# All input projections of the later batches in the first sixteen steps of a Mamba recurrence

## The reference

```python
zxbcdt = x @ in_proj_w.T            # 512 -> 2688 = z 1024, x 256, B 256, C 1024, dt 128
dt = softplus(dt_in @ dt_proj_w.T + dt_proj_b)
dA = exp(dt[..., None] * A)         # 1024 channels x 16 states
def step(h, inp):                   # over 512 tokens
    h = dA_i * h + dBx_i            # dBx = dt * x * B
    y = einsum('bgn,bgcn->bgc', C_i, h)
y = (ys + D_skip * x_full) * silu(z)
return y @ out_proj_w.T
```

## Time and profile before

| | us |
|---|---|
| median of 3 runs (lowest, highest) | 2873.14 (2871.67, 2876.65) |
| the profiled execution | 2876.27 |
| its span in the trace | 2874.5 |
| busy PE / DVE / ACT / POOL | 2651.7 / 2129.6 / 1152.1 / 1255.9 |
| recurrence, first to last scan's end | 78.05 to 1062 |

### The profile page before, as it was taken

One profiled execution on the slowest core, in us unless ns is written; L12 is line 12 of the kernel. 1 busy time (PEld: TensorE's weight loads), 2 busy tenths in 40 slices (PEclk: granted clock), 3 DMA queues, 4 the chain that ended last, 5 costly groups with the idle time before them and its releaser, 6 DMA issues.

```text
span 2874.5 us, 32445 instructions
## 1 busy us (share of the span) xinstructions
PE 2651.7 (92%) x11096; PEld 1880.8 (65%) x11096; DVE 2129.6 (74%) x2731; ACT 1152.1 (40%) x1690; POOL 1255.9 (44%) x836
## 2 busy tenths in 40 slices
PE   7888888888899878999999999999989999999999
PEld 3443444444344326788887777887877788888887
DVE  4999999999999985543366677777767865555563
ACT  4555555555555534432244443443333322222221
POOL 2789888888889871110010023222212522222220
PEclk8998998989889769999999999999999999999999
DMA  6654654554465436221111112112111111111111
GB/s 230 209 157 121 188 157 121 157 166 129 132 183 154 133 99 231 81 76 49 52 66 59 45 37 67 44 45 67 44 37 45 44 49 48 51 45 52 50 47 66
DMA packets 152310, 275.35 MB, mean 96 GB/s; under 512 B 27345, under 2 KB 27857, under 8 KB 151633
## 3 DMA queue, kind: packets, MB, share of 16 engines
q1 hardware_dynamic: 152144, 273.27, 31.5%
HBM read 178.01 MB, written 61.34 MB: 83 GB/s over the span
## 4 chain that ended last, share of the span: by engine, by line
PE 71%; DVE 11%; ACT 9%; issue 5%; POOL 2%; DMA 1%; SPq 1%; DVEq 0%; POOLq 0%; ACTq 0%
PE ps L1733 19%; PE ps L1734 18%; PE ps L1735 18%; PE ps L1772 8%; DVE state L1358 6%; ACT ps L847 5%; PE ps L1784 4%; POOL read L1172 1%; DMA uraw<-y_d 1%; PE ps L1924 1%; PE ps L1868 1%; PE ps L1898 1%; DVE drive L1349 1%; DVE act_o L1677 0%; POOL xhr L1217 0%
## 5 line engine op out<-in xcount | busy, mean ns | idle before, releaser
L1172 POOL TENSOR_TENSOR read<-state,c_t 128x512 f32<-128x512 f32 x512 | 664.0, 1308 | 138.2 <-DVE state L1358 118.5
L1358 DVE TENSOR_TENSOR_SCAN state<-ps,drive 128x512 f32<-128x512 f32 x512 | 622.3, 1216 | 14.3 <-ACT ps L847 12.8
L1733 PE MATMUL ps<-xh,ghi 128*128 128x512 f32 x1536 | 609.1, 397 | 5.7 <-issue 5.7
L1231 POOL TENSOR_TENSOR wdeq<-packed,scales 128x1024 f32<-128x1024 f16 x96 | 260.2, 2711 | 798.3 <-DVE packed L1510 798.3
L1735 PE MATMUL ps<-xh,glo 128*128 128x512 f32 x1536 | 599.3, 390 | 0.0
L1734 PE MATMUL ps<-xl,ghi 128*128 128x512 f32 x1536 | 599.2, 390 | 0.0
L847 ACT ACTIVATE ps<-ps,a_exp 128x512 f32<-128x512 f32 x512 | 338.9, 662 | 473.8 <-PE ps L1772 472.5
L1772 PE MATMUL ps<-dpack,sel 128*128 128x512 f32 x512 | 260.9, 510 | 114.2 <-DVE state L1358 112.1
L1677 DVE TENSOR_TENSOR act_o<-act_o,ps 128x512 f32<-128x512 f32 x192 | 131.7, 686 | 313.4 <-PE ps L1735 298.5
L1349 DVE TENSOR_TENSOR drive<-ps,b_t 128x512 f32<-128x512 f32 x512 | 344.1, 672 | 12.7 <-PE ps L1772 11.9
L1099 ACT ACTIVATE ahi<-act_o 128x512 fp32r<-128x512 f32 x192 | 121.4, 632 | 562.6 <-DVE act_o L1677 562.6
(11 more groups left out here) (204 smaller groups left out, 3775.3 us busy)
## 6 DMA issues: line engine op xcount, KB each, us to landing
whi<-w_d SPq DMA_DIRECT2D x63, 256.0 KB, 4.1
wlo<-w_d SPq DMA_DIRECT2D x63, 256.0 KB, 4.6
dpack<-dh SPq DMA_DIRECT2D x64, 128.0 KB, 3.8
dpack<-dl SPq DMA_DIRECT2D x64, 128.0 KB, 3.6
b_d<-ev SPq DMA_DIRECT2D x32, 256.0 KB
x_d<-ev SPq DMA_DIRECT2D x32, 256.0 KB, 2.6
vpack<-vh SPq DMA_DIRECT2D x64, 128.0 KB, 3.5
vpack<-vl SPq DMA_DIRECT2D x64, 128.0 KB, 2.8
```

What stands on the lines that cost most here:

```text
L1172: pool.tensor_tensor(read[:, n % RRING, :], state[:, n % SRING, :], c_t[:, g % 2, :], ALU.mult).then_inc(read_ready, 1)
L1231: pool.tensor_tensor(wdeq[:, :].rearrange("p (h n) -> p h n", h=2), codes, scale, ALU.mult).then_inc(deq, 1)
L1358: dve.tensor_tensor_scan(state[:, n % SRING, :], ps[:, n % 2, :], drive[:, n % DRING, :], 0.0, ALU.mult, ALU.add)\
L1733: pe.matmul(out_, w_h, x_h, start=(start and k == 0), stop=False)
```

## The change

`step_jobs` now gives each of the steps 0 to 15 five jobs, counted through all batches: step g has jobs 6 + 5g to 10 + 5g, step 15 the last three. Job i of a step is done in a slot of three states, 3i to 3i+2, with one, one and two feature blocks (`slot_of`); only state 15 has none. `take` comes in the state after the slot, `w_high` in its second and `w_low` in its third. In SP's order the five weight loads and spills (`weights`, `keep`) are put between the step's other loads. x is scaled and split for batches 1 to 3 in steps 1, 5, 9 and 2, 6, 10. Tile 0 of batches 1 to 3 goes the way of the others, through `ev` to DRAM (`dt_d`); SP loads it back into `dt_in` (`load_dt_in`), and ACT and DVE split it in steps 6, 14 and 22 (`take_dt`, `dt_split`). `sp_rest` takes the room of `sp_abs`, and `soft_abs` waits for `sp_sum_ready` in turn.

```diff
@@ -40,6 +40,9 @@
...
 STEPS = B * CT
+LEAD_JOBS, STEP_JOBS = 6, 5
+DT_STEP = tuple(CT * b - 2 for b in range(B))
+SCALE_STEP, SPLIT_STEP = (None, 1, 5, 9), (None, 2, 6, 10)
 IN_TILES = 21
@@ -108,10 +111,11 @@
...
     sp_abs = place("sp_abs", [P, S], F32, after())
+    sp_rest = place("sp_rest", [P, S], F32, offset_of["end"] - 4 * S)
     sp_pos = place("sp_pos", [P, S], F32, after())
...
     sp_log = place("sp_log", [P, S], F32, after())
-    sp_rest = place("sp_rest", [P, S], F32, after())
+    dt_in = place("dt_in", [P, S], F32, after())
     dt_t = place("dt_t", [P, S], F32, after())
@@ -202,6 +206,7 @@
...
     b_d = nc.dram_tensor("b_d", [CT, P, T], F32, kind="Internal").ap()
+    dt_d = nc.dram_tensor("dt_d", [P, T], F32, kind="Internal").ap()
     y_d = nc.dram_tensor("y_d", [CT, P, T], F32, kind="Internal").ap()
@@ -219,7 +224,8 @@
...
         consts_ready = sem("consts_ready")
-        x_loaded = [sem(f"x_loaded{b}") for b in range(B)]
+        x_loaded = [None] + [sem(f"x_loaded{b}") for b in range(1, B)]
+        dt_in_loaded = sem("dt_in_loaded")
@@ -355,19 +361,19 @@
...
-            nb, k = divmod(g + 2, CT)
-            return nb, k, nb < B and k < IN_TILES // 3
-        def spills(tile):
-            return 0 if tile == 0 else 4 if tile in (X0, B0, X1, B1) else 1
+            first = LEAD_JOBS + STEP_JOBS * g
+            return first, max(0, min(STEP_JOBS, IN_TILES * B - first))
+        def slot_of(c):
+            return divmod(c, 3) if c < 3 * STEP_JOBS else (STEP_JOBS, 0)
+        def spills(job):
+            return 0 if job == 0 else 4 if job % IN_TILES in (X0, B0, X1, B1) else 1
...
-            return 16 * sum(spills(j % IN_TILES) for j in range(job % 3, job + 1, 3))
-        def taken_count(job):
-            return job - job // IN_TILES
+            return 16 * sum(spills(j) for j in range(job % 3, job + 1, 3))
@@ -485,15 +491,17 @@
...
                 nb, tile = divmod(job, IN_TILES)
-                if tile == 0:
+                if job == 0:
                     return
-                sp.wait_ge(job_taken, taken_count(job))
+                sp.wait_ge(job_taken, job)
                 if tile in (X0, X1):
...
                     dsts = [b_copies[at:at + 8, rep, :, cols(nb)] for rep in range(4)]
+                elif tile == 0:
+                    dsts = [dt_d[:, cols(nb)]]
                 elif tile >= Z0:
@@ -525,13 +533,20 @@
...
-                sp.wait_ge(job_taken, taken_count(X0))
+                sp.wait_ge(job_taken, X0)
                 for e_ in range(4):
...
                 sp.dma_start(res_d[:, :, cols(b)], hat(b)).then_inc(res_stored, 16)
+            def load_dt_in(nb):
+                job = IN_TILES * nb
+                sp.wait_ge(spilled[job % 3], spill_count(job))
+                if nb >= 2:
+                    sp.wait_ge(dtlo_ready, nb)
+                sp.dma_start(dt_in[:, :], dt_d[:, cols(nb)]).then_inc(dt_in_loaded, 16)
@@ -616,8 +631,17 @@
...
             for g in range(STEPS):
-                nb, k, jobs = step_jobs(g)
-                first = IN_TILES * nb + 3 * k
+                first, jobs = step_jobs(g)
+                more = g + 1 < STEPS
+                def weights(i):
+                    if i < jobs:
+                        weights_after(first + i)
+                def keep(i):
+                    if i < jobs:
+                        spill(first + i)
                 if g == STEPS - 3:
@@ -626,27 +650,30 @@
...
                     store_hat(g // 2)
-                if 0 <= g + 1 < STEPS:
+                if g + 1 in DT_STEP[1:]:
+                    load_dt_in(DT_STEP.index(g + 1))
+                if more:
                     load_b(g + 1)
-                if jobs:
-                    weights_after(first)
-                    spill(first)
-                if 0 <= g + 1 < STEPS:
+                weights(0)
+                keep(0)
+                if more:
                     load_c(g + 1)
+                weights(1)
                 if g >= 1:
                     store_y(g - 1)
-                if jobs:
-                    weights_after(first + 1)
-                if 0 <= g + 1 < STEPS:
+                keep(1)
+                weights(2)
+                if more:
                     load_pack_dt(g + 1)
+                keep(2)
+                if more:
                     load_pack_v(g + 1)
-                if jobs:
-                    spill(first + 1)
+                weights(3)
+                keep(3)
                 if g + 2 < STEPS:
                     load_x(g + 2)
-                if jobs:
-                    weights_after(first + 2)
-                    spill(first + 2)
+                weights(4)
+                keep(4)
             store_y(STEPS - 1)
@@ -786,9 +813,7 @@
...
                 bank = ps[:, 5 + job % 2, :]
-                if tile == 0:
-                    if nb:
-                        act.wait_ge(dtp_ready, CT * nb)
+                if job == 0:
                     act.activation(dthi[:, :], bank, ACT.Copy).then_inc(dthi_ready, 1)
@@ -797,10 +822,16 @@
...
+            def take_dt(nb):
+                act.wait_ge(dt_in_loaded, 16 * nb)
+                act.wait_ge(dtp_ready, CT * nb)
+                act.activation(dthi[:, :], dt_in[:, :], ACT.Copy).then_inc(dthi_ready, 1)
             def soft_abs(q):
...
                     act.wait_ge(sp_exp_ready, q)
+                    act.wait_ge(sp_sum_ready, q)
                 act.activation(sp_abs[:, :], ps[:, 7, :], ACT.Abs, bias=dt_bias[:, q % CT:q % CT + 1])\
@@ -901,25 +932,27 @@
...
             for g in range(STEPS):
-                nb, k, jobs = step_jobs(g)
-                first = IN_TILES * nb + 3 * k
+                first, jobs = step_jobs(g)
                 for c in range(NST):
+                    i, part = slot_of(c)
                     decay(g, c)
                     for b in (1, 2, 3):
-                        if g == CT * b - 5 and c % 4 == 1:
+                        if g == SPLIT_STEP[b] and c % 4 == 1:
                             split_hi(b, c // 4)
+                        if g == DT_STEP[b] and c == 2:
+                            take_dt(b)
                     if g == STEPS - 3 and c >= 8 and c % 2 == 1:
                         out_weights_high((c - 8) // 2)
-                    if jobs and c % 4 == 2 and c < 12 and first + c // 4 + 2 < IN_TILES:
-                        w_high(first + c // 4 + 2)
-                    if jobs and c % 4 == 2 and c > 4:
-                        take(first + c // 4 - 1)
+                    if part == 0 and 1 <= i <= jobs:
+                        take(first + i - 1)
+                    if part == 1 and i < jobs and first + i + 2 < IN_TILES:
+                        w_high(first + i + 2)
                     if 0 <= g + 1 < STEPS:
...
                             v_high(g + 1)
-                    if nb < B:
+                    if g + 2 < STEPS:
                         if c == 12:
@@ -1327,7 +1360,7 @@
...
                 dve.wait_ge(dthi_ready, nb + 1)
-                dve.tensor_tensor(dtlo[:, :], ps[:, 5 + (IN_TILES * nb) % 2, :],
+                dve.tensor_tensor(dtlo[:, :], dt_in[:, :] if nb else ps[:, 5, :],
                                   dthi[:, :].bitcast(F32), ALU.subtract).then_inc(dtlo_ready, 1)
@@ -1409,26 +1442,26 @@
...
             for g in range(STEPS):
-                nb, k, jobs = step_jobs(g)
-                first = IN_TILES * nb + 3 * k
+                first, jobs = step_jobs(g)
                 for c in range(NST):
+                    i, part = slot_of(c)
                     if c + 1 < NST:
...
                     for b in (1, 2, 3):
-                        if g == CT * b - 6 and c % 4 == 1:
+                        if g == SCALE_STEP[b] and c % 4 == 1:
                             scale_x(b, c // 4)
-                        if g == CT * b - 5 and c % 4 == 2:
+                        if g == SPLIT_STEP[b] and c % 4 == 2:
                             split_lo(b, c // 4)
+                        if g == DT_STEP[b] and c == 5:
+                            dt_split(b)
                     if g >= 1 and c == 6:
                         skip_y(g - 1)
-                    if jobs and c % 4 == 3 and c < 12 and first + c // 4 + 2 < IN_TILES:
-                        w_low(first + c // 4 + 2)
-                    if nb and jobs and k == 0 and c == 6:
-                        dt_split(nb)
-                    if nb < B and c == 15:
+                    if part == 2 and i < jobs and first + i + 2 < IN_TILES:
+                        w_low(first + i + 2)
+                    if g + 2 < STEPS and c == 15:
                         soft_rest(g + 2)
@@ -1746,10 +1779,10 @@
...
                     if job >= 2:
-                        if (job - 2) % IN_TILES == 0:
-                            pe.wait_ge(dtlo_ready, nb + 1)
+                        if job == 2:
+                            pe.wait_ge(dtlo_ready, 1)
                         else:
```

(13 more changed lines are left out.)

## The result

| | kernel before | changed kernel |
|---|---|---|
| median (lowest to highest), 6 runs each | 2873.05 (2870.55 to 2876.65) | 2882.44 (2880.1 to 2888.81) |
| ratio, 95% interval | 1 | 1.0034 (1.0022 to 1.0046) |
| profiled execution, its span | 2876.27, 2874.5 | 2881.29, 2879.5 |
| DVE busy | 2129.6 | 2135.2 |
| recurrence: DVE waits | 27.2 | 25.9 |

The change costs 9.4 us, 0.3%. The two profiled executions are 5.0 us apart; from the first scan to the end of the last one the recurrence takes 4.2 us more (988.3 against 984.1).

A forecast was written before the change was run, and what follows sets the result against it. It took DVE to bound the recurrence, PE rearrangement being worth at most some 33 us. First stretch -0.6 (14.4 lost against 15) and second stretch +1 gave about 0, so 2873 us; range 2859 to 2888.

The forecast's parts named there:

- the bursts: Steps 3, 4, 7 and 8: four-fold X or B spills ahead of deadlines lose 8 us, between 2 and 18.
- the DVE work "kept" at nothing: Batches 1 to 3: scaling and splitting x keep their DVE cost and only change steps; nothing charged.
- the light steps: Steps 16 to 29, without projections: lose 16 us against 15 before, so +1 us, between -5 and +6.
- the step's floor of 28.68 us: One recurrence step on DVE: 14 states at 1.714 us, plus 2.37 (skip row) and 2.31 (softplus row).
- PE keeps up at five jobs, the clock holds: Steps 0 to 15: PE needs 27.1 us a step at full clock; a regular step stalls 0.14 us.
- Rival D: Clock falls in state 15 all the same, so the next step's start stalls; slower, 2882 us, chance 0.08.
- v's load in regular steps: Load of v for the next step, its deadline 1.4 us earlier: 0.2 us x 12 steps = 2.4 us lost.
- edits taken at nothing: Small changes charged no time, among them the dt tile's trip through DRAM, moved x work, new waits and sp_rest.
- two deadlines: DMAs queued behind SP: the load of v for the next step, and the weights of the step's fifth tile.
- second slow gather: Light steps: half have a second, making 1.5 us a step instead of 0.74; 1.15 taken.
- the 15 regained: Steps 0 to 15: PE's gain from removing stalls, 12.4 us idle and some 2.5 hidden.
- light steps at full clock: Rival E: spreads alone keep PE's clock up in steps without projections; faster, about 2857 us, chance 0.02.

The follow-up runs named there:

- e3: Changed kernel plus three matmuls without use in every state that has no projection in steps 15 to 31; 2872.07 us.
- e4: Kernel before, with its own schedule, plus three matmuls without use in every state that has no projection; 2844.98 us.
- e7: Changed kernel with four jobs a step instead of five, so steps 0 to 19 have projections in states 0 to 11; 2888.51 us.
- e1: Changed kernel with x and B tiles of batches 1 to 3 stored once, not four times, leaving part of the output wrong; 2867.76 us.
- e6: Changed kernel with x's scaling and splitting moved to late states and the split of dt to state 13 of the step before; 2879.79 us.
- e5: Kernel before with three useless matmuls in every state without a projection, and x's scaling and splitting moved to late states; 2842.39 us.

## Why the prediction was wrong

It gave 2873, no change, 42%; slower by over 0.2% had 28%. The time lies in its range, but it is slower. Two terms of the sum failed on the slow side: the bursts, put at 8 us, cost 17.5, and the DVE work "kept" at nothing took 5.1 more. A third, the light steps, failed on the other side and hid 7 us of that. By its own steps:

- **What bounds the recurrence, and the step's floor of 28.68 us: right.** Undisturbed steps of e3 and e4 take 28.65 to 28.66.
- **PE keeps up at five jobs, the clock holds: right.** Predicted 0.14 us of stall in a regular step; steps 11 and 12 take 28.77 and 28.83. Rival D (the clock falls in state 15) is out, and that its 2882 is the measured time is chance. In e7 four states without a projection are enough to bring the stall back in twelve of twenty steps; nothing between one and four was run.
- **v's load in regular steps, 2.4 us: too high.** It cost nothing there.
- **The bursts, 8 us within 2 to 18: the mechanism right, the size wrong.** They cost 17.5, at the far end. Steps 3 and 4 cost 9.5, not 6: issues behind the stores took longer too (1.2 and 2.1 us for 0.6). Steps 7 and 8 were to lose 2 at v's load and lost almost nothing there (0.2). But steps 8, 9 and 13 lost 8.0 at a deadline that the prediction didn't list: the weights for tiles 1 and 2 of the next step, behind the four-fold spills of jobs 3 and 4 (tiles are counted from 0 within a step). In step 13 the load of `dt_in`, one of the edits taken at nothing, stands in front as well. How much of the 2.9 us is its own no run separates; e1 leaves it in and has no wait there. The prediction named two deadlines of five; every load of the step stands behind some spill. e1 shows that the waits come from the four-fold stores: without them they are gone.
- **"Scaling and splitting keep their DVE cost": wrong.** DVE's busy time grew by 5.1 us, against nothing in the sum. The page's busy shares of DVE and GpSimd were both read, but not what they do to each other. The term was there to be read: scaling took 852 to 1095 ns in the kernel before, and takes 724 in e6's late states, where GpSimd is idle. That these 5.1 us count in full in the time is not shown: e6, which took part of them away, was faster by less than the intervals can tell.
- **Light steps, +1 us: wrong in sign.** They were put at 1.15 us a step, half of them with a second slow gather, and cost some 0.6: in five of fourteen only hidden tenths of a microsecond, in the other nine one stall after state 4, never one after state 12. The stretch lost some 9 us where it had lost 15 before. The second slow gather was a guess drawn from the last two steps.

With the measured terms the sum comes out near the traces' difference. First stretch: 2 (regular steps, as predicted), 0 (v), 17.5 (bursts) and about 1 (steps 0 to 2) are lost against the 15 regained: +5.5. DVE's longer work: +5.1. Second stretch: 9 lost instead of 15, -6. Together +4.6, where the recurrence took 4.2 us more of the traces' 5.0. The other 4 us of the medians' 9.4 are not explained; the changed kernel's six runs spread over 9 us, its profiled one among the faster.

Two slips in the recorded sums decide nothing: 3.18 - 1.72 - 1.0 + 0.3 is 0.76, not 0.74, and rival D's terms give +8, not +9.

Of the rival rules: the Trainium skill's page "TensorE: Matmul & The Clock Gate", section "The HAM clock gate", had light steps at full clock as long as the array is not idle. Steps 16 to 29 ran at 0.73 with a spread about every microsecond (PE busy 332.5 of 411.1 us, its longest gap 1.4 us); the measurement decides against that reading, and with e3's fill, which changes only the work that PE is given, the same steps ran at 0.99.

## What to carry to other kernels

Where PE's granted clock falls between two dense stretches and the next one starts with a stall, matmuls without use in a free bank can be the cheap repair: here some 600 of them (11,688 matmuls in the trace for 11,096) gave 1.1%, while moving the real work gave back at the DMA queue what it won at the array. Before work is packed denser, list for every load with a deadline what the issuing queue puts ahead of it in each step, the four-fold stores above all, and not only for the load that is tight today. And read an engine that is full for instructions whose length varies: here that was where another engine held it up.

## What the runs showed of the hardware

- DVE instructions that read both operands from SBUF take 0.66 to 0.72 us while GpSimd is idle, and up to 2.48 us behind GpSimd's reads in e5 (437.06), 3.01 in e6 (303.27). The longest is the scaling in step 5 of e1: GpSimd works without a gap from before its start (245.18) to 251.40, in five instructions; the scaling ends at 251.95, after 6.51 us. Whoever begins first holds the other up: GpSimd's read took 1.65 us instead of 1.27. The same subtraction with one operand in PSUM took 0.69 us in the midst of GpSimd's work, with both in SBUF 1.32. This agrees with the Trainium skill, page "SBUF — State Buffer", section "Who interferes with whom": a VectorE instruction with two SBUF inputs contends with a GpSimd instruction that reads SBUF, and the port pair that the two share is an exclusive lock.
- On SP the issue of a 128 KB DMA, mostly 0.46 to 0.6 us, took up to 2.14 us behind four stores of 256 KB, but also 1.66 us in e1 behind a single one.
- After four states with only spreads PE's granted clock is down (0.54 from 607 to 613 us); three matmuls without use in each held it at 0.99 (e4), where the kernel before has 0.87 over the recurrence.
